# Two changes to the attention heads of a four-layer kernel: causal masks added by products over 64 rows, and the out-projection as three f16 products

## The chip, the cores and the metric

One core of a Trainium2 chip (trn2). The metric is the device time of one execution in microseconds (us), lower is better. Three executions of the kernel before took 819.79, 821.60 and 822.36 us, median 821.6.

## The reference

x has 8 batches of 512 tokens of 128 features in f32. Four layers, each with a residual:

- x = x + A(norm(x)): causal attention of one head over 1,024 features
- x = x + F(norm(x)): an FFN through 64 channels with 16 inner units each
- x = x + B(norm(x)): `y = x + heads @ Wo`, with 16 heads of 64 features, `softmax(causal(q k^T / 8)) v`; then y is normalised, times gamma plus beta
- x = x + F(norm(x)) again

The change is in B. Its scores are masked above the diagonal, and its 1,024 head features are multiplied by Wo (1,024 x 128).

## The kernel before

P = 128 tokens make a block, so a batch has 4 row blocks. The kernel has two parts. The **front** (0 to about 180 us) runs A and the first F in a loop over b, software-pipelined: `front_tensor`, `front_scalar`, `front_vector` and `front_gpsimd` each hold one engine's order. The weights of B are prepared inside it: at b = 6 VectorE takes the largest absolute value of wv_b (`largest_vector`, L284); at b = 7 it scales wv_b down and wo_b up by the same number (`scale_weights_vector`, L301 and L303), so that v times wo needs no correction; at b = 8 ScalarE and VectorE split the weights of q, k and v in a high and a low part (L290 to L313). At b = 9 VectorE goes on with xt_lo (L532), and TensorE's products L399/L401 and VectorE's L449 come after it.

The **heads** (180 to about 785 us) are a loop over 64 pairs (b, p): batch b, heads 2p and 2p+1. Each pair has three units: unit 0 is row blocks 0 and 1, unit 1 is row block 2, unit 2 is row block 3. Every engine walks the same list of turns (b, p, s) with s = 0, 1, 2; the order inside a turn is written out by hand, and semaphores join the engines:

- TensorE (`heads_tensor`): scores of unit s (`pair_scores`): f32 products over 64 features for each of the two heads (L866), the heads on partitions 0 to 63 and 64 to 127, then for each row block and head one product of the identity with a triangle of -3e38, over 128 rows, in bf16 (L871). Then the probabilities times v of an older unit (`pair_values`, L891 to L893, f16, three products for each block). At s = 0 also the next pair's queries and the out-projection of the pair three back (`output_tensor`, L912: f32, one product for each of 4 blocks, recorded as two instructions each); at s = 1 the next pair's keys and the turning of the context of the pair two back (L185); at s = 2 values of the next batch and, at the batch's edges, products for the second F.
- VectorE (`heads_vector`): the row maxima of unit s (L1000), a sum of the second F (L1129), then the f16 cast of the probabilities of the unit before (L988); at s = 0 also the context times 1/sum (L1020) and v_lo (L821). For p = 2 to 5 it has norm work of the batch before.
- ScalarE (`heads_scalar`): the exponentials of unit s (L957); then q_sb at s = 0 (L842), ctx_t (L967) and k_sb (L848) at s = 1, v_hi at s = 2 (L817), and an activation of the second F (L1210).
- GpSimd (`heads_gpsimd`): for each unit the low half of the probabilities, f32 minus f16 to f16 (L1050), and behind it the small work of the second F and of the norms (`back_gpsimd`: L1147, L1155, L1096 to L1099, L1168), for the batch before.
- SP (`heads_sync`): for each unit two transposing DMAs, of the high half (L1065, waits for the cast) and of the low half (L1068, waits for GpSimd); `pair_values` waits for both.

PSUM bank YA collects the out-projection over the 8 pairs of a batch; `back_sum_vector` (L1080) adds it to the residual at (b + 1, p = 2). After the last pair a drain of 19 more turns finishes the pipeline. The f32 matrix products appear in the trace with their passes as separate instructions.

## Time and profile before

| | us |
|---|---|
| median of 3 executions | 821.6 (819.79 to 822.36) |
| the profiled execution | 822.15 |
| its span, first to last instruction | 820.3 |
| TensorE busy | 729.3 (89%) |
| VectorE busy | 624.9 (76%) |
| ScalarE busy | 559.2 (68%) |
| GpSimd busy | 518.6 (63%) |

The profiled execution is one of its own; durations and spans below are from it. PE is TensorE's products, PEld its weight loads, DVE VectorE, ACT ScalarE, POOL GpSimd, SPq the issues of SyncE. "L912" is line 912 of the kernel. A product's recorded length holds its passage through the array, so the pace of a row of products is read from their starts, or from the length of a merged row: its count less one, times the pace, plus the length of one. "<-" in brackets names what ended an idle time.

### The profile page before, as it was taken

The numbers are of one execution on the slowest core, as the hardware profiler recorded it, in microseconds if no ns is written. First come the engines' busy times: TensorE is split into PE (matmuls) and PEld (weight loads), VectorE is DVE, ScalarE is ACT, GpSimd is POOL, SyncE is SP. The second block draws the span as 40 slices with busy tenths as digits, with TensorE's granted clock in tenths as the row PEclk, the third lists the DMA queues.
The fourth block names the chain that finished last, engine by engine and source line by source line (L and its number), as shares of the span: only waits on it lengthen the run. The fifth ranks groups of instructions, "written<-read, shape, count | busy, mean of one in ns | idle before, by whom it ended". The sixth has DMA issues, their size and how long they took to land. (4 is left out here: it accounts for less than half of the span.)

```text
span 820.3 us, 20955 instructions
## 1 busy us (share of the span) xinstructions
PE 729.3 (89%) x7594; PEld 520.7 (63%) x7594; DVE 624.9 (76%) x1291; ACT 559.2 (68%) x1551; POOL 518.6 (63%) x496
## 2 busy tenths in 40 slices
PE   4899885569999999999999999999999999999742
PEld 3667664455776666766776677767666766676531
DVE  1578886557666887699789868987997798789963
ACT  1478775547767667777777777777777777776643
POOL 4558876226666668577657856785677568577821
PEclk9999998689999999999999999999999999999965
DMA  7500000007889877988867887877787689877820
GB/s 190 136 1 1 1 2 1 0 0 132 147 143 155 152 142 141 142 143 140 141 145 150 142 142 147 145 137 145 149 148 138 137 139 150 151 151 149 143 57 13
DMA packets 360614, 94.00 MB, mean 115 GB/s; under 512 B 347584, under 2 KB 360384, under 8 KB 360512
## 3 DMA queue, kind: packets, MB, share of 16 engines
q1 hardware_dynamic: 357248, 90.57, 60.7%
q10 hardware_dynamic: 3264, 2.10, 0.9%
q8 instruction: 61, 1.00, 0.6%
q14 instruction: 41, 0.34, 0.2%
HBM read 6.63 MB, written 2.10 MB: 11 GB/s over the span
## 5 line engine op out<-in xcount | busy, mean ns | idle before, releaser
L1050 POOL TENSOR_TENSOR prob_hl<-prob,prob_hl 128x768 f16<-128x768 f32 (+1 forms) x192 | 347.4, 1810 | 192.5 <-DVE prob_hl L988 192.2
L957 ACT ACTIVATE prob<-wide,neg_max 128x128 f32<-128x128 f32 (+3 forms) x512 | 264.1, 524 | 156.7 <-DVE neg_max L1000 156.6
L1000 DVE TENSOR_REDUCE neg_max<-wide 128x2 f32<-128x256 f32 (+3 forms) x256 | 204.6, 820 | 109.3 <-PE wide L871 108.7
L866 PE MATMUL wide<-k_sb,q_sb 64*128 64x128 f32 (+3 forms) x1024 | 190.1, 469 | 0.9 <-ACT k_sb L848 0.8
L988 DVE CAST prob_hl<-prob 128x768 f16<-128x768 f32 (+1 forms) x192 | 154.2, 803 | 0.6 <-ACT prob L957 0.5
L891 PE MATMUL bank<-v_hi,prob_t 128*128 128x64 f16 x1280 | 132.7, 193 | 13.4 <-DMA prob_t<-prob_hl 11.5
L893 PE MATMUL bank<-v_hi,prob_t 128*128 128x64 f16 x1280 | 132.7, 193 | 0.0
L892 PE MATMUL bank<-v_lo,prob_t 128*128 128x64 f16 x1280 | 132.7, 193 | 0.0
L891 PEld LDWEIGHTS bank<-v_hi,prob_t 128*128 128x128 f16 x1280 | 115.5, 98 | 20.4 <-issue 12.9
L893 PEld LDWEIGHTS bank<-v_hi,prob_t 128*128 128x128 f16 x1280 | 114.2, 98 | 0.0
L892 PEld LDWEIGHTS bank<-v_lo,prob_t 128*128 128x128 f16 x1280 | 114.1, 98 | 0.0
L957 ACT ACTIVATION_READ_ACCUMULATOR prob<-wide,neg_max 128x1 f32 x512 | 102.4, 200 | 0.0
L866 PEld LDWEIGHTS wide<-k_sb,q_sb 64*128 64x128 f32 x1024 | 72.1, 185 | 42.1 <-issue 33.3
L871 PEld LDWEIGHTS wide<-mask_bf,ident_bf 128*128 128x128 bf16 x512 | 29.0, 97 | 104.6 <-issue 104.6
L912 PEld LDWEIGHTS bank<-wo_up,ctx_t 128*128 128x128 f32 x512 | 66.7, 191 | 5.6
L912 PE MATMUL bank<-wo_up,ctx_t 128*128 128x128 f32 x512 | 67.6, 275 | 0.0
L871 PE MATMUL wide<-mask_bf,ident_bf 128*128 128x128 bf16 x512 | 62.0, 223 | 0.0
L424 ACT ACTIVATE ffn_relu<-ffn_s,b,w 128x512 f32<-128x512 f32 x64 | 50.1, 816 | 16.7 <-PE bank L401 13.5
L1210 ACT ACTIVATE relu_two<-ffn_s,b,w 128x512 f32<-128x512 f32 x64 | 52.8, 827 | 2.5 <-DVE ffn_g L1129 1.5
L1129 DVE SCALAR_TENSOR_TENSOR ffn_g<-relu_two,w,ffn_g 128x512 f32<-128x512 f32 x56 | 48.6, 868 | 1.1 <-ACT relu_two L1210 0.2
L1020 DVE TENSOR_TENSOR ctx_sb<-bank,rsum 128x512 f32<-128x512 f32 x64 | 40.8, 637 | 5.0 <-PE bank L893 5.0
L967 ACT COPY ctx_t<-bank 128x512 f32<-128x512 f32 x64 | 37.3, 582 | 4.7 <-PE bank L185 4.7
(169 smaller groups left out, 1314.9 us busy)
## 6 DMA issues: line engine op xcount, KB each, us to landing
prob_t<-prob_hl SPq DMA_TRANSPOSE x384, 2.8
x_sb<-in_L_attn_a_in_features SPq DMA_DIRECT2D x8, 256.0 KB, 5.6
out_x<-x_done SPq DMA_DIRECT2D x8, 256.0 KB, 2.5
wq_a<-in_L_attn_a_w_q ACTq DMA_DIRECT2D x1, 512.0 KB, 5.4
wk_a<-in_L_attn_a_w_k ACTq DMA_DIRECT2D x1, 512.0 KB, 7.1
wo_a<-in_L_attn_a_w_o ACTq DMA_DIRECT2D x1, 512.0 KB, 8.0
wv_a<-in_L_attn_a_w_v ACTq DMA_DIRECT2D x1, 512.0 KB, 8.1
wq_b<-in_L_attn_b_Wq SPq DMA_DIRECT2D x1, 512.0 KB, 9.7
```

Of the source, the lines that this page charges most:

```text
L424: act.activation(ffn_relu[:, j % RELUS, :], ffn_s[:, :], ACT.Relu, bias=b1_2[:, j:j + 1], scale=w1_2[:, j:j + 1]).then_inc(sem("f_relu"), 1)
L866: pe.matmul(dst[:, h, c:c + m], q[e, i * P:(i + 1) * P], k[e, 0:m], start=(i == UNIT_ROWS[u][0]), stop=False)
L871: last = pe.matmul(dst[:, h, c:c + P], ident_bf[:, :], mask_bf[:, :], start=False, stop=(i == UNIT_ROWS[u][-1]))
L891: pe.matmul(dst, prob_t[u][:, h * m + k, :], hi, start=(j == 0), stop=False)
L892: pe.matmul(dst, prob_t[u][:, h * m + k, :], lo, start=False, stop=False)
L893: last = pe.matmul(dst, prob_t[u][:, (2 + h) * m + k, :], hi, start=False, stop=(j == i))
L912: last = pe.matmul(YA[:, i * P:(i + 1) * P], ctx_t[:, i * P:(i + 1) * P], wo_up[:, p, :], start=(p == 0 and i == 0), stop=(p == HP - 1 and ...
L957: last = act.activation(prob_2[s][:, at:at + m], score_banks(p, s)[:, h, c:c + m], ACT.Exp, bias=neg_max[p % 2][:, h, i:i + 1], accum_out= ...
L988: dve.tensor_copy(prob_hl[u][:, 0:w], prob_2[u][:, 0:w]).then_inc(sem(f"ph{u}"), 1)
L1000: last = dve.tensor_reduce(neg_max[p % 2][:, :, i:i + 1], score_banks(p, s)[:, :, c:c + m], AX.X, ALU.max, negate=True)
L1050: pool.tensor_tensor(prob_hl[u][:, w:2 * w], prob_2[u][:, 0:w], prob_hl[u][:, 0:w], ALU.subtract)\
L1210: act.activation(relu_two[:, j % 2, :], ffn_s[:, :], ACT.Relu, bias=b1_2[:, j:j + 1], scale=w1_2[:, j:j + 1]).then_inc(sem("g_relu"), 1)
```

## The change

- The mask of a row block and head, one product over 128 rows, becomes two over 64 rows: one adds the triangle to all 128 columns for the upper 64 query rows, one to the last 64 columns for the lower 64. Head 0 takes them from partitions 0 to 63, head 1 from 64 to 127, out of a shifted identity and a wider triangle. The masks of the front keep 128 rows.
- wo_b gets its own largest value and is scaled by it, then split in an f16 high half (ScalarE) and an f16 low half (VectorE); the product of both scales comes back in the addition that reads YA.
- The context is copied from PSUM to f32 as before; ScalarE then copies that to f16 from SBUF, behind k_sb; GpSimd makes the f16 low half of it behind unit 0's L1050; the out-projection is hi x hi, hi x lo, lo x hi, and waits for the low half.
- The transposes and the start of the heads wait for the split of wo_b in place of its scaling.

```diff
@@ -83,8 +83,8 @@
         ident = sb("ident", [P, P])
-        ident_bf = sb("ident_bf", [P, P], BF16)
-        mask_bf = sb("mask_bf", [P, P], BF16)
+        shift_bf = sb("shift_bf", [P, 2 * P], BF16)
+        mask_bf = sb("mask_bf", [P, P + E], BF16)
...
@@ -108,11 +108,13 @@
-        wo_up = sb("wo_up", [P, HP, P])
-        largest = sb("largest", [P, 1])
+        wo_hi = sb("wo_hi", [P, HP, P], F16)
+        wo_lo = sb("wo_lo", [P, HP, P], F16)
+        y_scale = sb("y_scale", [P, 1])
+        largest = sb("largest", [P, 2])
         mean_of_rows = sb("mean_of_rows", [P, P])
-        scale_up = sb("scale_up", [P, 1])
-        scale_down = sb("scale_down", [P, 1])
+        scale_up = sb("scale_up", [P, 2])
+        scale_down = sb("scale_down", [P, 2])
@@ -144,6 +146,8 @@
         ctx_t = sb("ctx_t", [P, S])
+        ctx_t_hi = sb("ctx_t_hi", [P, S], F16)
+        ctx_t_lo = sb("ctx_t_lo", [P, S], F16)
@@ -160,7 +164,7 @@
                           stop=False)
             for i in UNIT_ROWS[u]:
                 c = PAIR_AT[i] + i * P
-                last = pe.matmul(dst[:, c:c + P], ident_bf[:, :], mask_bf[:, :], start=False,
+                last = pe.matmul(dst[:, c:c + P], shift_bf[:, E:E + P], mask_bf[:, 0:P], start=False,
                                  stop=(i == UNIT_ROWS[u][-1]))
             return last
@@ -217,28 +221,28 @@
         def prepare_gpsimd(pool):
             pool.memset(ident[:, :], 0.0).then_inc(sem("const_0"), 1)
-            pool.memset(ident_bf[:, :], 0.0).then_inc(sem("const_0"), 1)
+            pool.memset(shift_bf[:, :], 0.0).then_inc(sem("const_0"), 1)
             pool.memset(mask_bf[:, :], 0.0).then_inc(sem("const_0"), 1)
...
             pool.wait_ge(sem("const_0"), 7)
-            for m in (ident, ident_bf):
-                pool.affine_select(out=m[:, :], in_=m[:, :], compare_op=ALU.not_equal, fill=1.0, base=0,
-                                   pattern=[[-1, P]], channel_multiplier=1).then_inc(sem("consts"), 1)
+            for m, n, base in ((ident, P, 0), (shift_bf, 2 * P, E)):
+                pool.affine_select(out=m[:, :], in_=m[:, :], compare_op=ALU.not_equal, fill=1.0, base=base,
+                                   pattern=[[-1, n]], channel_multiplier=1).then_inc(sem("consts"), 1)
             pool.affine_select(out=mask_bf[:, :], in_=mask_bf[:, :], compare_op=ALU.is_ge, fill=MASKED, base=0,
-                               pattern=[[-1, P]], channel_multiplier=1).then_inc(sem("consts"), 1)
+                               pattern=[[-1, P + E]], channel_multiplier=1).then_inc(sem("consts"), 1)
...
         def scale_tensor(pe):
-            pe.wait_ge(sem("largest"), 1)
+            pe.wait_ge(sem("largest"), 2)
             pe.wait_ge(sem("mean_of_rows"), 1)
             pe.wait_ge(sem("at_g"), B)
-            pe.matmul(GX[:, 0:1], mean_of_rows[:, :], largest[:, :], start=True, stop=True).then_inc(sem("scale_ps"), 1)
+            pe.matmul(GX[:, 0:2], mean_of_rows[:, :], largest[:, :], start=True, stop=True).then_inc(sem("scale_ps"), 1)
         def prepare_tensor(pe):
             pe.wait_ge(sem("consts"), 3)
@@ -283,6 +287,8 @@
             dve.wait_ge(sem(LOADED_B), ALL_B)
             dve.tensor_reduce(largest[:, 0:1], wv_b[:, :, :], AX.XY, ALU.max, apply_absolute_value=True)\
                 .then_inc(sem("largest"), 1)
+            dve.tensor_reduce(largest[:, 1:2], wo_b[:, :, :], AX.XY, ALU.max, apply_absolute_value=True)\
+                .then_inc(sem("largest"), 1)
         def split_weights_scalar(act):
             act.wait_ge(sem(LOADED_B), ALL_B)
@@ -291,17 +297,20 @@
                     .then_inc(sem("wqk_hi"), 1)
             act.wait_ge(sem("wv_b_scaled"), 1)
             act.copy(wv_b_hi[:, :], wv_b[:, :, :]).then_inc(sem("wv_b_hi"), 1)
+            act.wait_ge(sem("wo_b_scaled"), 1)
+            act.copy(wo_hi[:, :, :], wo_b[:, :, :]).then_inc(sem("wo_hi"), 1)
         def scale_weights_vector(dve):
             dve.wait_ge(sem("scale_ps"), 1)
-            dve.tensor_scalar_max(scale_up[:, :], GX[:, 0:1], TINY).then_inc(sem("scale_up"), 1)
+            dve.tensor_scalar_max(scale_up[:, :], GX[:, 0:2], TINY).then_inc(sem("scale_up"), 1)
             dve.wait_ge(sem("scale_up"), 1)
             dve.reciprocal(scale_down[:, :], scale_up[:, :]).then_inc(sem("scale_down"), 1)
             dve.wait_ge(sem("scale_down"), 1)
             dve.tensor_scalar(wv_b[:, :, :], wv_b[:, :, :], scale_down[:, 0:1], None, ALU.mult)\
                 .then_inc(sem("wv_b_scaled"), 1)
-            dve.tensor_scalar(wo_up[:, :, :], wo_b[:, :, :], scale_up[:, 0:1], None, ALU.mult)\
-                .then_inc(sem("wo_up"), 1)
+            dve.tensor_scalar(wo_b[:, :, :], wo_b[:, :, :], scale_down[:, 1:2], None, ALU.mult)\
+                .then_inc(sem("wo_b_scaled"), 1)
+            dve.tensor_tensor(y_scale[:, :], scale_up[:, 0:1], scale_up[:, 1:2], ALU.mult).then_inc(sem("y_scale"), 1)
         def split_weights_vector(dve):
             for k, (w, parts) in enumerate(((wq_b, wq_parts), (wk_b, wk_parts))):
@@ -312,6 +321,9 @@
             dve.wait_ge(sem("wv_b_scaled"), 1)
             dve.tensor_tensor(wv_b_lo[:, :], wv_b[:, :, :].rearrange("p h e -> p (h e)"), wv_b_hi[:, :].bitcast(F32),
                               ALU.subtract).then_inc(sem("wv_b_lo"), 1)
+            dve.wait_ge(sem("wo_hi"), 1)
+            dve.wait_ge(sem("wo_b_scaled"), 1)
+            dve.tensor_tensor(wo_lo[:, :, :], wo_b[:, :, :], wo_hi[:, :, :], ALU.subtract).then_inc(sem("wo_parts"), 1)
         class Norm:
@@ -867,9 +879,13 @@
                               stop=False)
             for i in UNIT_ROWS[u]:
                 c = PAIR_AT[i] + i * P
-                for h in range(2):
-                    last = pe.matmul(dst[:, h, c:c + P], ident_bf[:, :], mask_bf[:, :], start=False,
-                                     stop=(i == UNIT_ROWS[u][-1]))
+                done = i == UNIT_ROWS[u][-1]
+                for r in range(2):
+                    for h in range(2):
+                        e = slice(h * E, (h + 1) * E)
+                        place = slice((1 - r + h) * E, (1 - r + h) * E + P)
+                        last = pe.matmul(dst[:, h, c + r * E:c + P], shift_bf[e, place],
+                                         mask_bf[e, h * E:h * E + P - r * E], start=False, stop=done and r == 1)
             last.then_inc(sem(f"s{u}"), 1)
         def pair_values(pe, b, p, u):
@@ -903,14 +919,17 @@
         def output_tensor(pe, b, p):
             n = number(b, p)
-            wait(pe, "ctx_t", n + 1)
+            wait(pe, "ctx_t_lo", n + 1)
             if n == 0:
                 wait(pe, "bn_xt_lo", B)
             if p == 0:
                 wait(pe, "y_acc", b)
             for i in range(QB):
-                last = pe.matmul(YA[:, i * P:(i + 1) * P], ctx_t[:, i * P:(i + 1) * P], wo_up[:, p, :],
-                                 start=(p == 0 and i == 0), stop=(p == HP - 1 and i == QB - 1))
+                block = slice(i * P, (i + 1) * P)
+                pe.matmul(YA[:, block], ctx_t_hi[:, block], wo_hi[:, p, :], start=(p == 0 and i == 0), stop=False)
+                pe.matmul(YA[:, block], ctx_t_hi[:, block], wo_lo[:, p, :], start=False, stop=False)
+                last = pe.matmul(YA[:, block], ctx_t_lo[:, block], wo_hi[:, p, :], start=False,
+                                 stop=(p == HP - 1 and i == QB - 1))
             last.then_inc(sem("y_ps"), 1)
         def heads_tensor(pe, b, p):
@@ -964,9 +983,13 @@
                 if s == 1 and pair_exists(*earlier(b, p, 2)):
                     wait(act, "ctx_t_ps", n - 1)
                     wait(act, "y_ps", n - 2)
+                    wait(act, "ctx_t_lo", n - 2)
                     act.copy(ctx_t[:, :], MB[:, :]).then_inc(sem("ctx_t"), 1)
                 if s == 1 and pair_exists(*later(b, p)):
                     keys_scalar(act, *later(b, p))
+                if s == 1 and pair_exists(*earlier(b, p, 2)):
+                    wait(act, "ctx_t", n - 1)
+                    act.copy(ctx_t_hi[:, :], ctx_t[:, :]).then_inc(sem("ctx_t_hi"), 1)
                 if s == 2 and b < B - 1:
                     values_scalar(act, b + 1, p, MB)
                 if s == 2 and (b, p) == (0, 1):
@@ -1043,15 +1066,26 @@
         def heads_gpsimd(pool, b, p):
             n = number(b, p)
+
+            def context_lower(u):
+                if u == 0 and pair_exists(*earlier(b, p, 2)):
+                    wait(pool, "ctx_t_hi", n - 1)
+                    wait(pool, "ctx_t", n - 1)
+                    wait(pool, "y_ps", n - 2)
+                    pool.tensor_tensor(ctx_t_lo[:, :], ctx_t[:, :], ctx_t_hi[:, :], ALU.subtract)\
+                        .then_inc(sem("ctx_t_lo"), 1)
+
             if pair_exists(b, p):
                 for u in range(NU):
                     w = 2 * unit_width(u)
                     wait(pool, f"ph{u}", n + 1)
                     pool.tensor_tensor(prob_hl[u][:, w:2 * w], prob_2[u][:, 0:w], prob_hl[u][:, 0:w], ALU.subtract)\
                         .then_inc(sem(f"pl{u}"), 1)
+                    context_lower(u)
                     back_gpsimd(pool, b, p, u)
             else:
                 for u in range(NU):
+                    context_lower(u)
                     back_gpsimd(pool, b, p, u)
         def heads_sync(sp, b, p):
@@ -1059,11 +1093,11 @@
             if pair_exists(b, p):
                 for u in range(NU):
                     m = 2 * len(unit_blocks(u))
-                    sp.wait_ge(sem("wo_up"), 1)
+                    sp.wait_ge(sem("wo_parts"), 1)
                     wait(sp, f"ph{u}", n + 1)
                     wait(sp, f"pv{u}", n)
                     sp.dma_start_transpose(prob_t[u][:, 0:m, :], prob_hl[u][:, 0:m * P]).then_inc(sem(f"pt_hi{u}"), 16)
-                    sp.wait_ge(sem("wo_up"), 1)
+                    sp.wait_ge(sem("wo_parts"), 1)
                     wait(sp, f"pl{u}", n + 1)
                     sp.dma_start_transpose(prob_t[u][:, m:2 * m, :], prob_hl[u][:, m * P:2 * m * P])\
                         .then_inc(sem(f"pt{u}"), 16)
@@ -1077,7 +1111,9 @@
             wait(dve, "y_ps", HP * (c + 1))
             wait(dve, "bn_y", B)
             tokens = y_res[:, seq(c), :]
-            dve.tensor_tensor(tokens, YA[:, :].rearrange("p (a d) -> p a d", d=P), tokens, ALU.add)\
+            wait(dve, "y_scale", 1)
+            dve.scalar_tensor_tensor(out=tokens, in0=YA[:, :].rearrange("p (a d) -> p a d", d=P),
+                                     scalar=y_scale[:, 0:1], in1=tokens, op0=ALU.mult, op1=ALU.add)\
                 .then_inc(sem("y_acc"), 1)
         def back_statistics(dve, norm, src, done, c):
@@ -1250,7 +1286,7 @@
                 if b == SCALE_STEP + 1:
                     scale_tensor(pe)
             pe.wait_ge(sem("wqk_lo"), 2)
-            pe.wait_ge(sem("wo_up"), 1)
+            pe.wait_ge(sem("wo_parts"), 1)
             project_tensor(pe, 0, 0, wq_parts, "q_ps")
             project_tensor(pe, 0, 0, wk_parts, "k_ps")
             pe.wait_ge(sem("v_lo"), VSLICES)
```

## Rows read from the trace of the kernel before

**Rows 1.** Windows: us, then busy (instructions) of PE, PEld, DVE, ACT, POOL; clock, DMA

```profile
60.00:184.00 124.00, 90.78 (x544) 71.44 (x542) 88.45 (x272) 79.55 (x151) 75.11 (x140) 0.88 0.00 1
240.00:740.00 500.00, 493.22 (x5679) 346.59 (x5678) 412.50 (x742) 371.90 (x1117) 341.70 (x229) 1.00 0.80 144
```

**Rows 2.** Windows inside the head stage, same columns

```profile
222.70:258.50 35.80, 35.80 (x423) 25.20 (x422) 24.05 (x42) 25.29 (x80) 21.69 (x12) 1.00 0.87 144
397.50:426.60 29.10, 28.92 (x328) 20.47 (x327) 20.83 (x36) 21.80 (x65) 16.26 (x9) 1.00 0.74 148
426.60:473.60 47.00, 46.06 (x532) 32.10 (x531) 42.78 (x80) 35.54 (x106) 35.71 (x26) 1.00 0.82 147
```

**Rows 3.** Waits of 240 to 740 us: who waited for whom; us in total, times, longest

```profile
POOL prob_hl L1050 <- DVE prob_hl L988: 157.5, 132, 3.0
...
DVE neg_max L1000 <- PE wide L871: 86.4, 105, 1.9
...
PE bank L891 <- DMA prob_t<-prob_hl: 4.3, 8, 1.2
```

**Rows 4.** Timeline of PE in one pair: start us, length us, line, operation, form, count

```profile
454.99 0.40 PE L871 MATMUL wide<-mask_bf,ident_bf 128*128 128x128 bf16 x4
...
456.94 1.05 PE L912 MATMUL bank<-wo_up,ctx_t 128*128 128x128 f32 x8
457.93 0.92 PE L866 MATMUL wide<-k_sb,q_sb 64*128 64x384 f32 x4
458.78 0.28 PE L871 MATMUL wide<-mask_bf,ident_bf 128*128 128x128 bf16 x2
458.90 0.19 PE L891 MATMUL bank<-v_hi,prob_t 128*128 128x64 f16 x1
```

**Rows 5.** Groups by line and form: count, busy us, mean ns, idle before

```profile
L912 PE MATMUL bank<-wo_up,ctx_t 128*128 128x128 f32 x512 | 67.6, 275 | 0.0
...
L871 PE MATMUL wide<-mask_bf,ident_bf 128*128 128x128 bf16 x512 | 62.0, 223 | 0.0
...
L817 ACT CAST v_hi<-bank 128x512 f16<-128x512 f32 x60 | 34.9, 583 | 0.2
...
L1155 POOL TENSOR_TENSOR ffn_xb<-x_ffn,bout_sb 128x512 f32<-128x512 f32 x8 | 11.1, 1393 | 2.0 <-DVE x_ffn L1116 2.0
```

**Rows 6.** Timeline of POOL, a calm pair and two busy ones; in brackets idle before

```profile
232.25 1.64 POOL L1050 TENSOR_TENSOR prob_hl<-prob,prob_hl 128x768 f16<-128x768 f32 x1 [1.64 <-DVE prob_hl L988]
234.67 2.13 POOL L1050 TENSOR_TENSOR prob_hl<-prob,prob_hl 128x1024 f16<-128x1024 f32 x1 [0.78 <-DVE prob_hl L988]
237.90 1.64 POOL L1050 TENSOR_TENSOR prob_hl<-prob,prob_hl 128x768 f16<-128x768 f32 x1 [1.11 <-DVE prob_hl L988]
...
534.10 2.14 POOL L1050 TENSOR_TENSOR prob_hl<-prob,prob_hl 128x1024 f16<-128x1024 f32 x1 [0.63 <-DVE prob_hl L988]
...
543.98 2.14 POOL L1050 TENSOR_TENSOR prob_hl<-prob,prob_hl 128x1024 f16<-128x1024 f32 x1
```

**Rows 7.** Timeline of ACT in a calm pair

```profile
230.05 0.60 ACT L848 COPY k_sb<-bank 128x512 f32<-128x512 f32 x1
231.74 0.69 ACT L957 ACTIVATE prob<-wide,neg_max 128x512 f32<-128x512 f32 x1 [1.09 <-DVE neg_max L1000]
```

**Rows 8.** Line 988 in 240 to 740 us: ns min/median/max, first and last start, forms

```profile
L988 DVE CAST prob_hl<-prob x161: 542/554/1856, 240.6 to 739.8; 128x768 f16<-128x768 f32 x107, 128x1024 f16<-128x1024 f32 x54
```

**Rows 9.** Timeline of DVE around the weights

```profile
116.25 1.19 DVE L284 TENSOR_REDUCE largest<-wv_b 128x1 f32<-128x1024 f32 x1
...
151.32 1.22 DVE L313 TENSOR_TENSOR wv_b_lo<-wv_b,wv_b_hi 128x1024 fp32r<-128x1024 f32 x1
...
158.73 0.69 DVE L449 TENSOR_TENSOR x_sb<-bank,ffn_xb 128x512 f32<-128x512 f32 x1 [5.58 <-PE bank L401]
```

**Rows 10.** Timeline of PE and DVE at the end of the heads

```profile
786.89 1.06 PE L912 MATMUL bank<-wo_up,ctx_t 128*128 128x128 f32 x8
...
790.60 0.68 DVE L1080 TENSOR_TENSOR y_res<-bank,y_res 128x512 f32<-128x512 f32 x1
```

## The prediction

> **What bounds the kernel now.** I read the windows by stage first [rows 1]. The reader is to see that the head stage (240 to 740 us) has TensorE busy 493 of 500 us at the full 2.4 GHz clock, while VectorE has 412, ScalarE 372 and GpSimd 342. The stage before it (60 to 184 us) has no engine near its full share: there a chain decides. A busy TensorE is not proof by itself, so I read finer windows next [rows 2]. Four pairs of heads from 222.7 us take 35.8 us, 8.94 each, with TensorE busy 35.80: these calm pairs run at TensorE's own pace. The first three pairs of a later batch (397.5 to 426.6 us) take 29.1, longer because whole products of the FFN stand in them, but TensorE is busy 28.9 of it: bound the same way. The last five pairs of a batch (426.6 to 473.6 us) take 47.0 us, 9.40 each. At TensorE's pace they would take 5 x 8.94, and about 0.44 for the four f32 products of 128 columns that turn the tokens at the batch's end, 45.1 in all: 1.9 us of waiting per batch. VectorE is busy 42.8 of those 47.0 us (8.56 a pair against 6.0 in a calm one) and GpSimd 35.7, because the residual, the norms and the FFN of the batch before are worked there. The waits say the same [rows 3]: GpSimd waits for VectorE's casts and VectorE waits for TensorE's masked scores; TensorE itself waits for the transposed probabilities 4.3 us in 8 places. So 64 pairs: all 8 of batch 0 and 3 of each of the 7 later batches are bound by TensorE (29), 35 are bound by TensorE and VectorE almost equally.
>
> **Out-projection, three f16 products.** Today eight f32 instructions run in a pair's turn: 1.05 us long, the last one 0.275, so a pace of 0.78 / 7 = 0.111 us and 0.89 in all [rows 4, 5]. The change issues twelve f16 products of 128 columns. No f16 product of 128 columns is in the trace; the nearest is the bf16 mask of 128 columns with its own weight load: four in 0.40 us, the last 0.22 long, 0.06 apart [rows 4, 5]. 128 columns at 2.4 GHz take 0.053, so 0.053 and 0.060 bound it; I take 0.056, hence 0.67, a gain of **0.22 us a pair** (0.17 to 0.25). The Trainium skill ("TensorE: Matmul & The Clock Gate", section Back-to-back issue gap) speaks against this: a stream of weight loads and products is said to hold about 81 ns apiece at 128 columns. The masks are such a stream and keep 0.06, so here row and rule differ; by the rule the twelve would take 0.97 and the gain would be gone (a rival below).
>
> **Masks over 64 rows.** Today a row of blocks costs two products over 128 rows, 2 x 0.056 = 0.11. The change makes four over 64 rows: two of 128 columns, two of 64, the two heads on separate halves. If the heads overlap, a row costs 0.056 + 0.029 = 0.085, 0.027 less, and four rows 0.11 less. That they overlap is shown by the scores: four f32 products of 384 columns (3 x 0.111 = 0.33 each, 1.33 in a line) start at 457.93 and the masks start 0.85 later, which is 2 x 0.33 and 0.19 for entering and leaving the 64-row form [rows 4]. The step out of the form costs about 0.1 of this; it stands before the masks today and behind them after, moved and not removed. For the smaller weight loads at the new place I take off 0.03: **0.08 us a pair** (from a loss of 0.24, no overlap, to a gain of 0.12). TensorE's total is then 0.30 us a pair, 19.2 us over 64.
>
> **ScalarE.** It adds one copy of 512 columns to f16. The f16 copy of the same size from PSUM takes 0.58 [rows 5]; I take that. It comes behind the copy of the keys, where a calm pair has 1.09 us idle before the next exponential, which waits for VectorE [rows 7]. Cost nothing in a calm pair; queued behind it is that exponential alone. If the cover goes, 0.5 a pair. The new wait of the ctx_t copy on GpSimd asks for a result about two units old: nothing.
>
> **GpSimd.** It adds one subtraction of 512 columns, f32 and f16 in, f16 out. A two-input f32 operation of 512 columns takes 1.39 [rows 5], the subtraction of 768 columns 1.64 and of 1024 2.13 [rows 6]; the step of 0.49 for 256 columns gives 1.15, which I take. It stands behind unit 0's subtraction, so unit 1's is queued behind it, and unit 1's low transposes on SP wait for that, then TensorE. It also waits for ScalarE's f16 copy: in a calm pair the keys are done at 230.65 [rows 7], so the copy at 231.2 and the subtraction from 231.3 to 232.4, beside a unit 1 that starts at 232.25 after 1.64 us idle: 0.2 late, and made up in the 0.78 before unit 2's and the 1.11 before the next unit 0's [rows 6]. Covered. Not in the pair at 538 us: there unit 0, a half of the tokens (L1168), unit 1, the other half and unit 2 follow one another, and unit 2's, from 543.98 to 546.12, has no idle time before it [rows 6]. Two such operations, in this pair and the one before it (0.63 us idle before its unit 2 [rows 6]), make unit 2's low half 1.7 us later. Transposes and the faster TensorE behind it have most of this in hand in some batches and not in others, so I put down 0.3 us per batch: **a loss of 2.0 us** over 7 (0 to 12).
>
> **VectorE beside a busier GpSimd.** The cast takes 0.55 us at the median and up to 1.86 [rows 8]; the long ones fall beside GpSimd's work. Another 1.15 us of GpSimd a pair, about half of it over a cast or an FFN sum, stretched by about half, costs some 0.3 us of VectorE. In calm pairs VectorE has 3 us free, so nothing. In the 35 busy pairs VectorE goes from 8.56 to 8.86 while TensorE's pace falls from 8.94 to 8.64: VectorE binds, and the gain does not come through. I take 0.05 a pair of it, **1.7 us** (none to 0.30 each). The calm 29 pass on all 0.30, **8.7 us**.
>
> **Weights.** wo_b now has its own largest value, its f16 high half and low half. The reduction of 1024 columns takes 1.19 and has the next step behind it 1.10 later; the low half is like L313, 1.22, of which 1.14 is path [rows 9]. Both are on VectorE in a chain: right behind the splits comes xt_lo, TensorE's next products wait for it, and VectorE then waits 5.58 us for those. The scaling of wo_b takes the place of wo_up's, same form. ScalarE's high half (about 1.05 us) lies beside VectorE's splits. y_scale and the wider tiny ops cost 0.15. **Cost 2.4 us** (1.2 to 3). The wider constants are made while the first tokens load: nothing.
>
> **The end.** The last out-projection ends at 787.95 and the sum that reads it starts at 790.60 [rows 10]: 2.65 us in hand, against a copy and a subtraction of 0.58 + 1.15 more before it. Covered; but the copy stands ahead of an FFN activation of the last but one batch, so I put down **0.3 us** (0 to 1.8). The sum over YA with its scale is one instruction as before.
>
> **Sum.** -8.7 - 1.7 + 2.0 + 2.4 + 0.3 = -5.7. The profiled execution took 822.15 us (span 820.3 and 1.85 around it), 0.55 above the median of 821.6. So 816.4 for such an execution, **816 us** on the median. A measurement of this kernel can tell 0.3%, 2.5 us, from no change.
>
> **Rivals.** (a) *TensorE alone counts* (0.20): the busy pairs pass on the 0.30 too, since VectorE still idles 4 us in five pairs: -19.2 + 2.7, 805 us. For it: TensorE 493 of 500. Against: the five-pair window. (b) *GpSimd's queue decides* (0.16), the slower case: in the 538 us pair unit 2's low half is 1.7 us late and TensorE's products with it wait the whole of it, 7 x 1.7 = 12, so -8.7 + 12 + 2.7 = +6, 828 us. It decides once unit 2's transposes have less than 1.7 us in hand; for it: TensorE has waited for transposes already [rows 3]; against: only 4.3 us of it. (c) *f16 products at the wider spacing* (0.04): were two 128-column products 0.08 apart, TensorE would gain nothing in sum; 0 + 2.7 + 2.0, 826 us. The page on TensorE in the Trainium skill named above states that spacing. (d) *the 64-row masks do not overlap* (0.07): 0.17 a row, 0.24 lost a pair, which cancels the out-projection's 0.22: 826 us. My forecast has 0.53.
>
> From these: faster by over 0.3%: 0.46 of my case and all of (a), 0.66. Same: 0.07, 0.04 of (b), 0.02 of (c) and (d), 0.13. Slower: 0.12 of (b), 0.09 of (c) and (d), 0.21. The range holds 8 in 10 from just above (a) to (c) and (d): 806 to 826. The likeliest case's own range is 810 to 820.
>
> **What would show it.** Right: a calm window of four pairs at 34.6 us; twelve out-projection products about 0.056 apart; masks in 64*128 form with the heads' starts nearly together; the five-pair window at 46.7 to 47; the VectorE cast's mean up; GpSimd's new operation near 1.15 us; the heads starting 2.3 us later. Wrong: calm pairs still at 8.9 (products or masks priced wrong), calm pairs bound by VectorE, the five-pair window at 45.5 or less (a) or over 48.5 with TensorE waiting for transposes of unit 2 (b).

## The result, and the profile after

The changed kernel takes **849.1 us** at the median (844.6 to 850.8) against 821.1 for the kernel before, measured beside it: ratio 1.032, interval 1.029 to 1.035. The forecast was 816 in 806 to 826. The profiled execution took 850.8 us, its span is 849.0.

First the windows of the changed kernel: us, busy time of PE, PEld, DVE, ACT, POOL, clock, DMA share, GB/s. They answer to [rows 1, 2].

```profile
60.00:184.00 124.00, 89.20 (x529) 71.59 (x527) 88.23 (x270) 78.35 (x142) 75.17 (x139) 0.85 0.00 1
240.00:740.00 500.00, 461.43 (x6058) 328.38 (x6055) 435.88 (x706) 386.41 (x1129) 394.98 (x272) 0.99 0.86 138
435.40:484.70 49.30, 44.16 (x590) 31.46 (x589) 45.44 (x80) 38.23 (x111) 41.81 (x31) 1.00 0.83 137
```

In the head stage TensorE was busy 493 of 500 us and is now busy 461: it has begun to wait. (The granted clock of 0.99 is 6.8 us at the lower level.) The last five pairs of a batch take 49.3 us where they took 47.0, with TensorE idle 5.1 of them. VectorE has 23 us more in the 500, though fewer of its instructions fall into them (706 against 742).

The starts of the first and of the last pair, in the timelines of TensorE, before and after:

```profile
179.73 0.93 PE L866 MATMUL wide<-k_sb,q_sb 64*128 64x128 f32 x8 [0.77 <-ACT k_sb L848]
763.64 0.93 PE L866 MATMUL wide<-k_sb,q_sb 64*128 64x128 f32 x8
```

```profile
184.28 0.93 PE L878 MATMUL wide<-k_sb,q_sb 64*128 64x128 f32 x8 [0.77 <-ACT k_sb L860]
...
789.07 0.93 PE L878 MATMUL wide<-k_sb,q_sb 64*128 64x128 f32 x8
```

They divide the 28.7 us between the spans: 4.6 before the heads, 20.9 in the 63 pairs from start to start (604.8 against 583.9), 3.3 behind the last start (59.9 against 56.6). Pair by pair, the 20.9 lie in few places: the eight pairs of batch 0 take 0.9 us less than before, the first three of the seven later batches together 0.5 more, and the last five of them 21.3 more, most of it in p = 4 (8.5) and p = 7 (8.1).

One calm pair of the changed kernel, timeline of TensorE (start, length):

```profile
426.82 0.93 PE L878 MATMUL wide<-k_sb,q_sb 64*128 64x128 f32 x8
427.58 0.34 PE L887 MATMUL wide<-mask_bf,shift_bf 64*128 64x128 bf16 x8
429.34 0.23 PE L929 MATMUL bank<-wo_hi,ctx_t_hi 128*128 128x128 f16 x1
...
429.96 0.22 PE L931 MATMUL bank<-wo_hi,ctx_t_lo 128*128 128x128 f16 x1
430.11 0.92 PE L878 MATMUL wide<-k_sb,q_sb 64*128 64x384 f32 x4
...
435.44 0.93 PE L878 MATMUL wide<-k_sb,q_sb 64*128 64x128 f32 x8
```

The pair takes 8.62 us, near the forecast of 8.64. The twelve products stand (429.96 - 429.34) / 11 = 0.056 apart. But the forecast's sign was four calm pairs in 34.6 us, and the four that stand where [rows 2] has its 35.80 take 36.60 here, 225.83 to 262.43: one of them takes 9.65, and two more 9.1 and 9.2. TensorE's work in a pair was priced right; what it won is lost elsewhere. The waits of 240 to 740 us tell where (us, times, longest), against [rows 3]:

```profile
POOL prob_hl L1082 <- DVE prob_hl L1011: 95.6, 104, 2.0
...
DVE neg_max L1023 <- PE wide L887: 60.8, 81, 2.5
...
PE bank L907 <- DMA prob_t<-prob_hl: 26.1, 33, 2.1
...
PE bank L907 <- DVE ctx_sb L1043: 9.6, 10, 1.5
POOL ctx_t_lo L1075 <- ACT ctx_t_hi L992: 7.9, 16, 0.8
```

TensorE waits for transposed probabilities 26 us in 33 places (before: 4.3 in 8) and for VectorE's scaling of the context (9.6 us in 10 places). GpSimd and VectorE wait less than before: they are the busier ones. The groups by form in the same stretch, which answer to [rows 5, 8]:

```profile
L1011 DVE CAST prob_hl<-prob 128x768 f16<-128x768 f32 x103 | 89.4, 868 | 0.0
...
L1165 DVE SCALAR_TENSOR_TENSOR ffn_g<-relu_two,w,ffn_g 128x512 f32<-128x512 f32 x35 | 37.0, 1056 | 0.0
...
L992 ACT CAST ctx_t_hi<-ctx_t 128x512 f16<-128x512 f32 x51 | 32.8, 644 | 0.0
...
L1075 POOL TENSOR_TENSOR ctx_t_lo<-ctx_t,ctx_t_hi 128x512 f16<-128x512 f32 x51 | 64.0, 1255 | 7.9 <-ACT ctx_t_hi L992 7.9
```

The two new operations cost near what was taken (0.644 for 0.58, 1.255 for 1.15). But the cast of 768 columns, the same instruction as before, has gone from 615 ns to 868 at the mean, and the FFN sum from 832 to 1056. How, the two timelines of VectorE and GpSimd show:

```profile
435.28 1.23 DVE L1011 CAST prob_hl<-prob 128x768 f16<-128x768 f32 x1
...
554.08 2.01 DVE L1011 CAST prob_hl<-prob 128x768 f16<-128x768 f32 x1
```

```profile
434.94 1.16 POOL L1075 TENSOR_TENSOR ctx_t_lo<-ctx_t,ctx_t_hi 128x512 f16<-128x512 f32 x1 [0.18 <-ACT ctx_t_hi L992]
...
554.03 1.64 POOL L1082 TENSOR_TENSOR prob_hl<-prob,prob_hl 128x768 f16<-128x768 f32 x1
555.64 1.47 POOL L1075 TENSOR_TENSOR ctx_t_lo<-ctx_t,ctx_t_hi 128x512 f16<-128x512 f32 x1
```

The cast at 435.28 ends at 436.51, which is 0.41 us behind the subtraction's end at 436.10; the one at 554.08 ends 0.42 behind the end, at 555.67, of the GpSimd instruction in which it began. These casts are not slowed in proportion, they are **held until a GpSimd instruction ends** and then take 0.42 us (0.55 with 1024 columns). I counted as held every cast of 240 to 740 us that is over 1.15 times its usual 550 or 683 ns: 46 of 161 before, 71 of 154 after. Every one of them, in both kernels, ends within 12 ns of 0.415 (768 columns) or 0.549 us (1024) behind the end of a GpSimd instruction. The FFN sum shows the same: 11 of 35 in the changed kernel, and 6 of 36 before, are over 1.15 times the usual 743 ns, and each of these ends 0.545 to 0.553 us behind the end of a GpSimd instruction. The Trainium skill (SBUF — State Buffer, section Who interferes with whom) says that a VectorE copy in its two-port mode and a GpSimd instruction take a shared port as an exclusive lock for a whole instruction. The trace agrees for these casts; for a GpSimd operation on few data it does not (n_masks_pow, below).

### The profile page after: what moved, and what is told of

Same layout as the page of the kernel before. It is cut to its first block and busy times, and to the rows that moved or that the text cites. A ratio compares the mean times of both kernels' runs of the same rounds, so it can differ in the third digit from the quotient of the medians.

```text
span 849.0 us, 22688 instructions
## 1 busy us (share of the span) xinstructions
PE 714.5 (84%) x8362; PEld 518.5 (61%) x8362; DVE 673.7 (79%) x1294; ACT 595.4 (70%) x1616; POOL 602.7 (71%) x560
## 3 DMA queue, kind: packets, MB, share of 16 engines
q1 hardware_dynamic: 357248, 90.57, 65.7%
## 5 line engine op out<-in xcount | busy, mean ns | idle before, releaser
L1082 POOL TENSOR_TENSOR prob_hl<-prob,prob_hl 128x768 f16<-128x768 f32 (+1 forms) x192 | 351.9, 1835 | 124.0 <-DVE prob_hl L1011 121.8
L1011 DVE CAST prob_hl<-prob 128x768 f16<-128x768 f32 (+1 forms) x192 | 179.0, 932 | 3.4 <-DMA prob_t<-prob_hl 2.5
L907 PEld LDWEIGHTS bank<-v_hi,prob_t 128*128 128x128 f16 x1280 | 112.7, 98 | 70.8 <-issue 39.8
L909 PEld LDWEIGHTS bank<-v_hi,prob_t 128*128 128x128 f16 x1280 | 114.5, 98 | 0.0
L1075 POOL TENSOR_TENSOR ctx_t_lo<-ctx_t,ctx_t_hi 128x512 f16<-128x512 f32 x64 | 80.0, 1251 | 17.2 <-ACT ctx_t_hi L992 17.2
L887 PEld LDWEIGHTS wide<-mask_bf,shift_bf 64*128 64x128 bf16 x1024 | 44.3, 94 | 67.8 <-issue 51.0
L1165 DVE SCALAR_TENSOR_TENSOR ffn_g<-relu_two,w,ffn_g 128x512 f32<-128x512 f32 x56 | 56.6, 1011 | 1.1 <-ACT relu_two L1246 0.2
L887 PE MATMUL wide<-mask_bf,shift_bf 64*128 64x128 bf16 (+1 forms) x1024 | 53.8, 203 | 0.0
L929 PE MATMUL bank<-wo_hi,ctx_t_hi 128*128 128x128 f16 x256 | 47.9, 224 | 1.4 <-POOL ctx_t_lo L1075 1.4
L930 PE MATMUL bank<-wo_lo,ctx_t_hi 128*128 128x128 f16 x256 | 47.2, 222 | 0.0
L931 PE MATMUL bank<-wo_hi,ctx_t_lo 128*128 128x128 f16 x256 | 47.2, 222 | 0.0
```

Of the source, the lines that this page charges most:

```text
L887: last = pe.matmul(dst[:, h, c + r * E:c + P], shift_bf[e, place], mask_bf[e, h * E:h * E + P - r * E], start=False, stop=done and r == 1)
L907: pe.matmul(dst, prob_t[u][:, h * m + k, :], hi, start=(j == 0), stop=False)
L909: last = pe.matmul(dst, prob_t[u][:, (2 + h) * m + k, :], hi, start=False, stop=(j == i))
L1011: dve.tensor_copy(prob_hl[u][:, 0:w], prob_2[u][:, 0:w]).then_inc(sem(f"ph{u}"), 1)
L1075: pool.tensor_tensor(ctx_t_lo[:, :], ctx_t[:, :], ctx_t_hi[:, :], ALU.subtract)\
L1082: pool.tensor_tensor(prob_hl[u][:, w:2 * w], prob_2[u][:, 0:w], prob_hl[u][:, 0:w], ALU.subtract)\
```

## The experiments

Differences between kernels are taken from the ratios to the kernel before on the same chip (1% is 8.2 us). The numbers of spans and groups are of the profiled executions.

**Layout.** The new tiles move prob_hl and prob_t off a multiple of 256 bytes; the share of the transposes' queue on the page of the profile rose from 60.7 to 65.7%. Two runs put this alone to the test.

```
 a_aligned (changed kernel)
+        pad = sb("pad", [P, 24])
         x_sb = sb("x_sb", [P, NT, P])
 b_shifted (kernel before)
+        pad = sb("pad", [P, 8])
         x_sb = sb("x_sb", [P, NT, P])
```

> The change with an unused tile of 96 bytes a partition ahead of x_sb, so that x_sb, prob_hl, prob_t and the rest up to the new f16 context start at the same offset within 512 bytes as in the kernel before; in the change prob_hl and prob_t start 160 bytes past a multiple of 256. Layout theory: the transposes' packets of 256 bytes, 18 ns at the median before and 20.7 ns in the mean in the change (10% of them 28 or more), are 18 again, TensorE's waits on transposes in 240 to 740 us fall from 26 us towards 4, and the time is 815 to 830. GpSimd theory (the subtraction of the context holds up the low halves and stretches VectorE's casts): packets may be quicker, but the time stays at 842 to 850.

> The kernel before with an unused tile of 32 bytes a partition ahead of x_sb: same instructions, x_sb, prob_hl and prob_t 32 bytes past a multiple of 256. Layout theory: packets of the transposes go from 18 ns to over 20, the calm pairs from 8.94 to 9.1 or more with TensorE waiting for transposes, and the time is 830 to 845. GpSimd theory: no change, 819 to 824.

a_aligned 847.1 us (1.029, 1.027 to 1.031), b_shifted 823.1 (1.000, 0.998 to 1.002). In the records the 256-byte packets that take under 60 ns have a mean of 18.0 ns where the tiles are aligned (kernel before, a_aligned) and 20.5 to 20.6 where they are not (b_shifted, changed kernel); the median is 18 in all four. The Trainium skill (DMA: Bandwidth & Descriptors, section How a descriptor splits into AXI transactions) has an unaligned piece cost extra, which agrees. The time hardly follows, and both runs came out as the expectation without a layout effect has it: layout is not the cause. What follows builds on a_aligned.

**One half each.** c_out_only has the old masks over 128 rows; d_masks_only is the kernel before with the new masks.

```
 c_out_only (on a_aligned)
-                for r in range(2): ... shift_bf[e, place], mask_bf[e, ...]
+                for h in range(2):
+                    last = pe.matmul(dst[:, h, c:c + P], shift_bf[:, E:E + P], mask_bf[:, 0:P], ...)
 d_masks_only (on the kernel before): the diff's lines on shift_bf, mask_bf and pair_scores alone
```

> The out-projection of the change alone, with the 96 bytes of a_aligned; the masks are products over 128 rows as before. Layout theory: 4 to 6 us over a_aligned, since calm pairs lose 0.09 us of TensorE. GpSimd theory: as a_aligned within 3 us, 845 to 852, since the waits are not TensorE's. If masks over 64 rows are themselves the cost, this run is well under a_aligned.

> The masks over 64 rows alone, at the offsets of the kernel before: f32 out-projection, no new work on ScalarE or GpSimd. Both theories: calm pairs 8.94 to 8.85, time 815 to 820. If more weight loads and products or their fetching cost something of their own, over 823.

c_out_only 850.6 (1.033, 1.031 to 1.035); **d_masks_only 814.2 (0.989, 0.986 to 0.991)**. The masks alone gain 1.15%, 9 us; the whole loss is in the out-projection. Beside the new out-projection the masks bring only 3 us (c_out_only against a_aligned, intervals that overlap), which fits with TensorE not deciding there. d_masks_only beats both kernels, by a little more than its expectation had. Its calm pairs take 8.81 us in place of 8.94 ("calm" is a pair in which no other engine holds TensorE up), as two starts of TensorE, two pairs apart, show:

```profile
238.77 0.93 PE L867 MATMUL wide<-k_sb,q_sb 64*128 64x128 f32 x8
...
256.40 0.93 PE L867 MATMUL wide<-k_sb,q_sb 64*128 64x128 f32 x8
```

**Parts of the out-projection.** In all of these the low half of the context is left out (h_dve_lo apart, which is whole), and the third product reads ctx_t_hi; in g_lo_no_wait it reads a subtraction of two tiles that never change.

```
 e_no_lo (on a_aligned)
-                    pool.tensor_tensor(ctx_t_lo[:, :], ctx_t[:, :], ctx_t_hi[:, :], ALU.subtract)
 f_narrow_lo
+                    pool.tensor_tensor(ctx_t_lo[:, 0:32], ctx_t[:, 0:32], ctx_t_hi[:, 0:32], ALU.subtract)
 g_lo_no_wait
-                    wait(pool, "ctx_t_hi", n - 1)
-                    pool.tensor_tensor(ctx_t_lo[:, :], ctx_t[:, :], ctx_t_hi[:, :], ALU.subtract)
+                    pool.tensor_tensor(ctx_t_lo[:, :], x_sb[...512 columns...], wo_lo[...], ALU.subtract)
 h_dve_lo: the subtraction in VectorE's turn 2, behind the cast of unit 1
+                    dve.tensor_tensor(ctx_t_lo[:, :], ctx_t[:, :], ctx_t_hi[:, :], ALU.subtract)
```

> a_aligned (847.1) without the subtraction on GpSimd: the third product of the out-projection reads the f16 high half again, in place of the low half, so TensorE's and ScalarE's work stay and the low half is left out of the result. GpSimd theory (its subtraction is the cost, by its place in the queue or by its time): the five-pair windows fall back below 47 us and the time to 808 to 818. ScalarE theory (the f16 copy of 0.65 us behind the keys delays exponentials): 835 or more.

> a_aligned with GpSimd's subtraction on 32 of the 512 columns, same place and same waits; the third product reads the high half, so the low half is left out of the result. If the new wait of GpSimd for ScalarE's copy, with unit 1's subtraction queued behind it, is the cost: 835 or more. If the 1.25 us of GpSimd's time are: within 5 us of e_no_lo.

> a_aligned with a subtraction of the same size and form on GpSimd that reads x_sb and wo_lo, which do not change in the heads, so that it needs not wait for ScalarE; the third product reads what it writes, so the result has no true low half. If GpSimd's time (and the VectorE casts stretched beside it) is the cost: 840 or more. If the wait for ScalarE is: 822 or less. Between them, each has its part.

> a_aligned with the low half of the context made by VectorE at turn 2 behind the cast of unit 1, about 0.65 us, GpSimd as in the kernel before. If VectorE's own load decides in the busy pairs, its 0.65 us cost as much as GpSimd's 1.25 did through stretched casts: 840 or more. If GpSimd's queue was the cost: 820 or less.

e_no_lo 820.3 (0.996, 0.993 to 0.999), f_narrow_lo 822.2 (0.999), g_lo_no_wait 843.2 (1.026, 1.022 to 1.029), h_dve_lo 828.3 (1.007, 1.005 to 1.009). From a_aligned to e_no_lo is 3.3%, **27 us for one GpSimd instruction a pair**. Its waits and the coupling alone cost little (f_narrow_lo 2 us above e_no_lo), the wait for ScalarE too (a_aligned 3 us above g_lo_no_wait, intervals that overlap). VectorE does the same work for 9 us, between what its two expectations had; e_no_lo came out 2 us above its range, f_narrow_lo and g_lo_no_wait as GpSimd's time had it.

**What in the GpSimd instruction costs.** i_pow is f_narrow_lo with a power over 128 by 4 elements in the subtraction's place: nearly as long (1.16 us in the mean against 1.24 in a_aligned), with hardly any data (low half left out). m_masks_extra and n_masks_pow add an instruction that nobody reads to d_masks_only, which has nothing of the new out-projection; s_extra_turn2 puts the idle subtraction at the end of the pair's three. The expectations count the units otherwise than the code: what they call behind unit 1 is `u == 0`, behind unit 0's low half, where the change has its subtraction; behind unit 2 is `u == 1`; the last of the pair is `u == 2`.

```
 i_pow
-                    pool.tensor_tensor(ctx_t_lo[:, 0:32], ctx_t[:, 0:32], ctx_t_hi[:, 0:32], ALU.subtract)
+                    pool.tensor_tensor(idle[:, :], ln_eps[:, :], rs_power[:, :], ALU.pow)
 m_masks_extra (on d_masks_only, behind unit 0's low half, u == 0)
+                        pool.tensor_tensor(idle[:, :], x_sb[...512 columns...], wo_up[...], ALU.subtract)
 n_masks_pow (the same place)
+                        pool.tensor_tensor(idle[:, :], ln_eps[:, :], rs_power[:, :], ALU.pow)
 s_extra_turn2 (on m_masks_extra)
-                    if u == 0:
+                    if u == 2:
```

> The subtraction of f_narrow_lo gives way to a GpSimd power over 128 by 4 elements (1.04 to 1.18 us in the trace of a_aligned), behind the same waits: as long as the subtraction of 512 columns (1.25), with hardly any traffic. The third product reads the high half; the low half of the context is left out. If the time that the instruction takes in GpSimd's queue is the cost (the next low half and its transposes come later), 840 to 847 us, and VectorE's casts are stretched as seldom as in f_narrow_lo. If the cost is that the wide subtraction holds up VectorE's casts, 820 to 826 us. If any GpSimd instruction holds them, whatever it moves, 840 to 847 with casts stretched as often as in a_aligned (71 of 155).

> d_masks_only (814.2 us, the old out-projection in one f32 product) and in each pair, behind the low half of unit 1, a GpSimd subtraction of 512 columns from two tiles that never change into a tile that nobody reads. Nothing of the change's out-projection is in it. If GpSimd's instruction alone is the cost: 834 to 842 us, as g_lo_no_wait stands 23 us above e_no_lo. If it needs the new out-projection beside it (ScalarE's copy, the later product): 814 to 820 us.

> d_masks_only and, in the place where m_masks_extra has its subtraction, the GpSimd power over 128 by 4 elements of i_pow (1.05 to 1.2 us, hardly any traffic). Two shares are told apart: if the instruction's time in GpSimd's queue costs what it does with the new out-projection (i_pow stands 13.0 us above f_narrow_lo), 825 to 830 us, and the rest of m_masks_extra's 32 us is the hold on VectorE. If the queue is nothing here: 814 to 818. If it is all: 840 to 846.

> m_masks_extra (846.3 us) with its idle subtraction behind unit 0's low half in place of unit 1's. If the place decides: 814 to 822 us, near d_masks_only (814.2). If every place costs: 835 to 846.

i_pow 835.2 us (1.018, 1.012 to 1.024), m_masks_extra 846.3 (1.030, 1.026 to 1.034), n_masks_pow 832.5 (1.012, 1.008 to 1.017), s_extra_turn2 841.0 (1.022, 1.019 to 1.025). i_pow lies between its expectations (its highest of four runs took 844.3), m_masks_extra 4 us and n_masks_pow 2.5 us above theirs. So the loss needs nothing of the out-projection: a subtraction that nobody reads costs 34 us over d_masks_only, in another place still 27. The power costs 19 of the 34 there, and 16 over f_narrow_lo where the subtraction costs 25: **more than half is time in GpSimd's queue, the rest (15 and 9 by difference) is put down to the hold on VectorE**. The split is rough: the subtraction of m_masks_extra is itself longer than the power, 1.38 us against 1.15 in the mean, and if the queue's part grows with that length it is 19 x 1.38 / 1.15 = 23 and the rest 11 (an estimate). Between 240 and 740 us VectorE's casts take 138 us in m_masks_extra and 124 in n_masks_pow, which bears the hold out; another effect of the wide instruction's data was not told apart from it.

The cost is not spread over the pairs. In batch 0, which has no work of a batch before it, the idle subtraction adds 0.4 us to eight pairs; in the seven later batches it adds 4.6 us at p = 0, 7.4 at p = 4, 5.8 at p = 5, 7.3 at p = 7, and 0.3 to 0.7 at each other place.

The two timelines of n_masks_pow, then of m_masks_extra, show a cast inside either instruction:

```profile
429.09 0.55 DVE L994 CAST prob_hl<-prob 128x768 f16<-128x768 f32 x1
```

```profile
428.53 1.15 POOL L1060 TENSOR_TENSOR idle<-ln_eps,rs_power 128x4 f32<-128x4 f32 x1
```

```profile
432.24 1.14 DVE L994 CAST prob_hl<-prob 128x768 f16<-128x768 f32 x1
```

```profile
431.67 1.29 POOL L1062 TENSOR_TENSOR idle<-x_sb,wo_up 128x512 f16<-128x512 f32 x1
```

Inside the power the cast takes its usual 0.55 us; inside the subtraction it ends 0.42 behind its end. Of the casts that begin inside the extra instruction, over 150 ns before its end, 0 of 21 were held in n_masks_pow, 0 of 38 in i_pow, and 33 of 34 in m_masks_extra. Here the measurement differs from the words "for the whole instruction" in the section of the Trainium skill named above (SBUF — State Buffer): a GpSimd instruction that works 1.0 to 1.5 us on four columns does not hold VectorE's casts. The waits of n_masks_pow, then of m_masks_extra, show the two ways into TensorE:

```profile
PE bank L897 <- DMA prob_t<-prob_hl: 20.2, 26, 2.1
...
PE bank L897 <- DVE ctx_sb L1026: 1.5, 3, 0.7
```

```profile
PE bank L897 <- DMA prob_t<-prob_hl: 18.9, 26, 2.2
...
PE bank L897 <- DVE ctx_sb L1026: 11.1, 12, 1.4
```

In d_masks_only the second of these rows does not occur, and the first is this; the row below it is that of e_no_lo:

```profile
PE bank L896 <- DMA prob_t<-prob_hl: 9.0, 16, 1.4
```

```profile
PE bank L908 <- DMA prob_t<-prob_hl: 19.3, 21, 2.2
```

So, as these rows read, the queue's part comes as late low halves and their transposes, the hold's part as VectorE's late context.

**The transposes.** In e_no_lo nothing of GpSimd's new work is left, and yet it is 6 us slower than d_masks_only. l_half_dma is e_no_lo without the transposes of the low halves (left out, the high one is read twice; context's low half left out too), q_lo_half_dma is a_aligned without them, and k_no_hi is e_no_lo with ScalarE's f16 copy straight from PSUM and no other.

```
 l_half_dma, q_lo_half_dma
-                    sp.dma_start_transpose(prob_t[u][:, m:2 * m, :], prob_hl[u][:, m * P:2 * m * P])
-            wait(pe, f"pt{u}", 16 * (n + 1))
+            wait(pe, f"pl{u}", n + 1)
 k_no_hi
-                    act.copy(ctx_t[:, :], MB[:, :]).then_inc(sem("ctx_t"), 1)
-                    act.copy(ctx_t_hi[:, :], ctx_t[:, :]).then_inc(sem("ctx_t_hi"), 1)
+                    act.copy(ctx_t_hi[:, :], MB[:, :]).then_inc(sem("ctx_t"), 1)
```

> e_no_lo without the transposes of the low halves of the probabilities; the value product reads the high transpose in their place, and TensorE and VectorE wait for GpSimd's subtraction instead of for the transpose. Left out: the low half's transposes, and the context's low half. TensorE's work is the same. If the queue of the transposes is what keeps the pairs above TensorE's pace of 8.62 us: the waits at the value products go, and the 64 pairs run at 8.7 to 9.0 us, 780 to 800 us in all. If the pairs hang on GpSimd and VectorE before the transposes are issued: 812 to 820 us.

> e_no_lo with ScalarE making the f16 copy straight from PSUM in place of the f32 copy, so its second copy (0.645 us a pair) and the wait for it are gone; the low half is left out and the third product reads the high half. If ScalarE's second copy is why e_no_lo (820.3) stays above d_masks_only (814.2) though its TensorE work is 0.22 us a pair less: 805 to 813 us. If the transposes bound the pairs anyway and ScalarE's copy lies beside them: 817 to 821 us.

> a_aligned with the true subtraction of the context, and without the transposes of the low halves of the probabilities, as l_half_dma (804.6 us); those are left out. If GpSimd's delay reaches TensorE through the transposes, which stand in one queue and take up to 1.33 us each, the subtraction costs little here: 805 to 812 us. If it costs the 27 us that it costs beside the full transposes: 828 to 834.

l_half_dma 804.6 (0.979, 0.976 to 0.981), k_no_hi 816.8 (0.993, 0.991 to 0.996), q_lo_half_dma 829.4 (1.009, 1.008 to 1.011). Half of the transposes away gives back 14 us, less than the 20 or more that its expectation had for a queue that decides; ScalarE's extra copy only 2, and those intervals overlap. Four calm pairs, which [rows 2] has at 35.80 and the changed kernel at 36.60, now take 34.58, the 34.6 of the forecast:

```profile
225.18 0.93 PE L879 MATMUL wide<-k_sb,q_sb 64*128 64x128 f32 x8
...
259.76 0.93 PE L879 MATMUL wide<-k_sb,q_sb 64*128 64x128 f32 x8
```

So without GpSimd's part the faster TensorE ran into the transposes. The timeline of SP's queue in e_no_lo, one pair, one start and length each:

```profile
299.19 2.45 SPq L1096 DMA_TRANSPOSE prob_t<-prob_hl  x1
301.73 1.24 SPq L1099 DMA_TRANSPOSE prob_t<-prob_hl  x1
303.07 1.25 SPq L1096 DMA_TRANSPOSE prob_t<-prob_hl  x1
304.41 1.26 SPq L1099 DMA_TRANSPOSE prob_t<-prob_hl  x1
305.77 1.23 SPq L1096 DMA_TRANSPOSE prob_t<-prob_hl  x1
307.09 1.24 SPq L1099 DMA_TRANSPOSE prob_t<-prob_hl  x1
308.44 2.82 SPq L1096 DMA_TRANSPOSE prob_t<-prob_hl  x1
```

Each starts 0.1 us behind the end of the last: the queue has no idle time here, and six take 9.25 us where TensorE needs 8.62. From 240 to 740 us its idle time beyond these 0.1 us adds up to 16 us in e_no_lo, 22 in d_masks_only, 36 in the kernel before and 53 in the changed kernel: there the queue itself waits more, which fits with GpSimd and VectorE being late. Of the 321 transposes of e_no_lo in this stretch, 48 take 1.85 to 2.97 us instead of 1.24 (33 of 319 before). During each of the 48 a packet of instruction fetch of 8 or 16 KB stands in the records of the DMA engines, and during 46 of the 263 that take 1.3 us or less; whether it is the cause was not tested. q_lo_half_dma stands 25 us above l_half_dma: GpSimd's subtraction costs the same without that queue, so of the two expectations the one by which its delay passes through the low transposes fell. In q_lo_half_dma TensorE (row of PE) waits 15.6 us for VectorE's context in 500 us, against 7.8 in l_half_dma, and 4.4 us in 6 places for the low half of the context.

**Another place or size, nothing left out.**

```
 o_lo_turn1: context_lower behind unit 1's low half
-                if u == 0 and pair_exists(*earlier(b, p, 2)):
+                if u == 1 and pair_exists(*earlier(b, p, 2)):
 p_lo_halves: 256 columns behind unit 0's low half, 256 behind unit 1's
+                if u < 2 and pair_exists(*earlier(b, p, 2)):
+                    c = slice(u * 256, (u + 1) * 256)
 r_lo_turn2: behind unit 2's (u == 2), output_tensor at s == 1 in place of s == 0
```

> The changed kernel (as a_aligned, 847.1 us) with the subtraction of the context behind unit 2's low half in place of unit 1's, one turn of GpSimd later; nothing is left out. If the cost is where it stands in the queue (the low half of unit 2, whose transpose TensorE waits for most, comes 1.25 us late): 830 to 838 us. If any place costs the same, because each turn has a cast that is held or a low half that is late: 844 to 850. If TensorE's out-projection now waits for it: 850 to 860.

> The changed kernel (as a_aligned) with the subtraction of the context as two of 256 columns, one behind unit 1's low half and one behind unit 2's; nothing is left out. If a hold on VectorE lasts to the end of the GpSimd instruction, each is about half as long (estimate 0.65 us) and the whole costs less: 836 to 843 us. If each of them costs a delay of its own: 847 to 855.

> The changed kernel (as a_aligned, 847.1 us) with the subtraction of the context behind unit 0's low half, the last of the pair, and the out-projection's twelve products moved one turn later on TensorE, ahead of the context's transposes; nothing is left out. If the cost is the place between two low halves: 816 to 826 us, near e_no_lo (820.3). If every place costs the hold on VectorE or the queue: 835 to 848. If the out-projection still waits for the low half: over 850.

o_lo_turn1 885.8 us (1.076), p_lo_halves 872.3 (1.061), r_lo_turn2 1040.5 (1.263): all far worse. The first two lie above every case of their expectations; the third is the case over 850, in which the out-projection waits for the low half. The waits of o_lo_turn1, then of r_lo_turn2:

```profile
PEld bank L930 <- POOL ctx_t_lo L1076: 70.8, 49, 2.6
PE bank L930 <- POOL ctx_t_lo L1076: 51.9, 35, 2.2
```

```profile
ACT ctx_t L988 <- PE bank L190: 125.2, 39, 4.7
PEld bank L930 <- POOL ctx_t_lo L1076: 99.3, 39, 3.5
PE bank L930 <- POOL ctx_t_lo L1076: 94.7, 39, 3.4
```

The out-projection now waits for the low half 35 to 39 times in 500 us; in p_lo_halves it is 35 times too, 49.4 us. In r_lo_turn2 the product stands ahead of TensorE's turning of the context, ScalarE waits for that (125 us) and its copies feed the next low half: by the order of the code these close a ring. TensorE is busy 397 of these 500 us there, and its granted clock is 0.90 in their mean, so a part of this time is a lower clock. So these runs measure that wait, and say of the place in GpSimd's queue only that the earliest is the best for this consumer. s_extra_turn2, which has no consumer, is the clean test: the place is worth 7 us of 34.

## Why the prediction was wrong

- **TensorE's terms held in their sum.** The products stand 0.056 us apart, as taken, and where nothing else holds TensorE a calm pair takes 8.62 to 8.65 for 8.64. The two terms in that sum missed in opposite ways, which is luck: the masks brought 0.13 us a pair (8.94 to 8.81) for 0.08, 9 us in all for 5; the out-projection 0.16 to 0.19 (8.81 to 8.65 or 8.62) for 0.22. Rivals (c) and (d) are out: d_masks_only is faster, and the 81 ns spacing that the Trainium skill states (TensorE: Matmul & The Clock Gate, section Back-to-back issue gap) does not hold in this stream.
- **"GpSimd: a loss of 2.0 us (0 to 12)" is the step that failed.** It measured 27. I asked whether GpSimd had idle time of its own in a calm pair and in the pair at 538 us, and charged one pair in each batch. For calm pairs the answer held (0.4 us in eight pairs of m_masks_extra). In the busy part of a batch GpSimd's idle times are waits for VectorE's next cast, no reserve, and the cost comes in several pairs of each batch (most at p = 0, 4, 5 and 7 in m_masks_extra; from e_no_lo to a_aligned at p = 0, 3, 5, 6 and 7), about 4 us a batch in place of 0.3. The queue's part alone (16 to 19 us by the power) is above my upper bound.
- **"VectorE beside a busier GpSimd", a gain of 1.7 us, was the wrong form.** I stretched overlapping casts by half. They are held until the GpSimd instruction ends (2.01 us for 0.55 at 554.08), and the mean of 768 columns went up by 253 ns. Rows 8 had shown 1856 against a median of 554; I read a slowdown in proportion where two timelines side by side would have shown a common end. By difference this hold is 9 to 15 us of GpSimd's cost.
- **"Calm 29 pairs pass on all 0.30, 8.7 us" failed too.** They passed on 0.4 us (0.9 less in batch 0, 0.5 more in the others). Of the out-projection's 14 us (0.22 x 64) nothing is left even without GpSimd's part: e_no_lo is 6 us slower than d_masks_only. The transposes on SP were back to back at 9 us a pair already in the calm pairs of the kernel before: there 25 steps from the start of one to the start of the next take 37.54 us (222.36 to 259.90), 9.0 for six. I read that GpSimd, VectorE and TensorE were near one another and left SP's queue out of the sum. TensorE's gain became its wait for transposes (9.0 us in d_masks_only, 19.3 in e_no_lo, in 500 us). l_half_dma gives 14 us back.
- **ScalarE's copy "covered"**: nearly (2 us, not told from nothing with certainty); the wait of GpSimd for it 3 us, not told from nothing either.
- **Weights 2.4: about right.** The heads start 1.2 us later in a_aligned and 4.6 in the changed kernel, with the same instructions; the 3 us between the two go with the granted clock. Of the first 178 us TensorE has 34.1 at the lower level of 1.2 GHz in the kernel before and in a_aligned, and 40.2 in the changed kernel, while it is busy 128 to 131 of them in all three. Among all runs with 34.1 the heads start at 178.7 and 179.7 us with the old weights and 180.5 to 181.8 with the new; with 40 to 41 at 181.3 and 181.4 against 183.4 to 184.3. So at an equal clock the weights cost about 2 us.
- **The end 0.3**: measured 3.3. GpSimd's last subtraction starts at 813.98 and the sum over YA follows at 819.12, behind FFN sums on VectorE that were held or queued (L1161 takes 1.51 us there for 0.55). The 2.65 us in hand were read of TensorE, not of VectorE. The granted clock was lower too, 0.68 against 0.71 behind the last pair's start; its share is open.
- **The rivals.** (b), at 0.16, went the right way, and what was to show it is there (a five-pair window over 48.5, here 49.3, with waits for transposes). Its price of 12 us for the queue is near the 16 to 19 measured, but by luck: it has one pair in each batch pay, the runs several; and it left the hold out. (a) fell.

What stays open: why the cost falls on these pairs of a batch, followed engine by engine; and a place for the low half at which it costs nothing, if there is one. The best whole kernel with the new out-projection, h_dve_lo at 828.3 us, is still slower than the masks alone.
